# Storing y from ACT's queue in place of SP's in a two-step conditional residual kernel

## The reference, cut to what matters

```
x: (128, 64, 1024) float32; cond ids: (128,) in 0..15; adapter ids: (128,) in 3..7
x = x + einsum('bct,bcd->bdt', x, W0[cond])       # W0[16]: 64 x 64 per condition
x = x + einsum('bsi,boi->bso', x, W1[adapter])    # W1[8]: 1024 x 1024 per adapter
```

## Time and profile before

| what | value |
|---|---|
| median of 3 runs | 861.83 us (860.33 to 862.73) |
| span of the profiled execution | 859.8 us |
| PE matmul | 813.6 us, 95% |
| DVE | 450.2 us, 52% |
| ACT | 279.4 us, 32% |
| POOL | 26.5 us, 3% |
| mean granted TensorE clock | 0.993 |
| DMAs | 90.84 MB, mean 106 GB/s |

### The profile page before, as it was taken

The page is one execution under the profiler, slowest core; times in us unless marked ns, Lnnn a source line. Parts: engine busy times, 40 slices in busy tenths (PEclk is TensorE's granted clock), DMA queues, the critical chain, the costliest instruction groups (busy, mean ns, idle before and its releaser), DMA issues.

```text
span 859.8 us, 17186 instructions
## 1 busy us (share of the span) xinstructions
PE 813.6 (95%) x3572; PEld 666.1 (77%) x3573; DVE 450.2 (52%) x466; ACT 279.4 (32%) x515; POOL 26.5 (3%) x61
## 2 busy tenths in 40 slices
PE   3599999999999999999999999999999999999997
PEld 3478778778777888877778887777888888888885
DVE  5556665566666344656653465666344433444342
ACT  2233233323323333233233323323333223322332
POOL 3100000000000000000000000000000000000000
PEclk9799999999999999999999999999999999999999
DMA  4433333334333323343333233333322322223223
GB/s 143 140 110 106 125 112 123 111 114 128 107 124 116 97 80 99 113 129 106 125 115 98 90 112 126 108 127 108 98 83 81 92 86 86 81 88 90 86 79 88
DMA packets 66655, 90.84 MB, mean 106 GB/s; under 512 B 6228, under 2 KB 57428, under 8 KB 66644
## 3 DMA queue, kind: packets, MB, share of 16 engines
q1 hardware_dynamic: 66644, 90.72, 34.2%
HBM read 57.15 MB, written 33.55 MB: 105 GB/s over the span
## 4 chain that ended last, share of the span: by engine, by line
PE 57%; SPq 18%; issue 7%; DVE 7%; ACT 3%; DMA 3%; DVEq 3%; ACTq 1%; POOL 0%; POOLq 0%
PE z_ps L452 17%; PE z_ps L453 17%; PE z_ps L455 16%; SPq L342 5%; SPq L191 5%; SPq L359 4%; DVE w_turned L700 3%; DVE x_turned L715 2%; SPq L373 2%; PE y_ps L466 2%; PE y_ps L468 2%; PE y_ps L467 2%; DVEq L191 2%; DMA w_nat<-in_L_cond_weight_dram 1%; DMA y<-in_L_cond_weight_dram 1%
## 5 line engine op out<-in xcount | busy, mean ns | idle before, releaser
L452 PE MATMUL z_ps<-w_hi,xt_hi 128*128 (+1 forms) x1056 | 413.3, 391 | 16.7 <-DVE z_lo L740 16.4
L453 PE MATMUL z_ps<-w_lo,xt_hi 128*128 (+1 forms) x1056 | 410.9, 389 | 0.0
L455 PE MATMUL z_ps<-w_hi,xt_lo 128*128 (+1 forms) x992 | 386.1, 389 | 0.0
L452 PEld LDWEIGHTS z_ps<-w_hi,xt_hi 128*128 128x128 f32 x1056 | 198.2, 188 | 66.2 <-issue 25.5
L453 PEld LDWEIGHTS z_ps<-w_lo,xt_hi 128*128 128x128 f32 x1056 | 198.3, 188 | 40.6
L455 PEld LDWEIGHTS z_ps<-w_hi,xt_lo 128*128 128x128 f32 x992 | 186.2, 188 | 38.9
L740 DVE TENSOR_TENSOR z_lo<-z_ps,z_hi 128x512 fp32r<-128x512 f32 x132 | 90.9, 689 | 201.2 <-ACT z_hi L559 200.6
L715 DVE STREAM_TRANSPOSE x_turned<-x_in 128x1024 f32<-128x1024 f32 x67 | 143.9, 2148 | 42.0 <-issue 31.7
L547 ACT ACTIVATE xt_hi<-x_turned 128x1024 fp32r<-128x1024 f32 x67 | 71.1, 1061 | 241.3 <-DVE x_turned L715 241.3
L559 ACT ACTIVATE z_hi<-z_ps 128x512 fp32r<-128x512 f32 x132 | 78.1, 592 | 191.3 <-PE z_ps L455 143.8
L724 DVE TENSOR_TENSOR xt_lo<-x_turned,xt_hi 128x1024 fp32r<-128x1024 f32 x62 | 76.7, 1236 | 69.9 <-ACT xt_hi L547 69.9
(11 more groups left out here) (111 smaller groups left out, 141.7 us busy)
## 6 DMA issues: line engine op xcount, KB each, us to landing
x_in<-in_x_dram SPq DMA_DIRECT2D x272, 128.0 KB
out_dram<-y SPq DMA_DIRECT2D x128, 256.0 KB, 3.1
w_nat<-in_L_cond_weight_dram SPq DMA_DIRECT2D x128, 128.0 KB
w_nat<-in_L_cond_weight_dram SPq DMA_DIRECT2D x4, 512.0 KB, 7.0
w_turned<-in_L_cond_weight_dram SPq DMA_DIRECT2D x2, 512.0 KB, 3.8
y<-in_L_cond_weight_dram SPq DMA_DIRECT2D x2, 512.0 KB, 8.3
x_turned<-in_L_cond_weights_dram SPq DMA_DIRECT2D x2, 256.0 KB, 3.9
ids_i<-in_itok_B_dram SPq DMA_DIRECT2D x2, 0.5 KB, 2.1
```

The lines of the kernel that those rows point to most:

```text
L452: nc.tensor.matmul(z_ps[n][:], xt_hi[h][:, t, :], whi, start=(t == 0), stop=False)
L453: mm = nc.tensor.matmul(z_ps[n][:], xt_hi[h][:, t, :], wlo, start=False, stop=last and not pair)
L455: mm = nc.tensor.matmul(z_ps[n][:], xt_lo[h][:, t, :], whi, start=False, stop=last)
```

## The change

`store_y` leaves SP's program. The same function, with the same look at three fields of the table, the same wait for `y_made` and the same two DMAs, is now issued by ACT as the last step of its slot, behind `keep_z_hi(s, 1)`, and once more behind the last `make_y`. The buffers, the semaphores and the order of everything else stay. SP waits for the last stores as before.

```
             def slot(j, h):
                 s = 2 * j + h
                 load_x(s + 2, h, turned=s + 1)
                 load_chunks(s + 1)
-                if not first:
-                    store_y(j - 1 + h, 1 - h)
...
-            store_y(pairs_past, 1)
...
+            def store_y(s, h):
+
+                a, b, stores = look(act, s, SAMPLE_A, SAMPLE_B, STORES)
+
+                def store(sample, lo):
+                    act.dma_start(out_rows[bass.ds(sample * C, C), :], y[h][lo:lo + C, :]).then_inc(y_stored[h], 16)
+
+                with act.If(stores > 1):
+                    act.wait_ge(y_made, NH * s + NH)
+                    store(a, 0)
+                    store(b, C)
...
                 make_y(before, 1 - h)
                 place_w0_a(s)
                 keep_z_hi(s, 1)
+                store_y(before, 1 - h)
...
             make_y(2 * pairs_past + 1, 1)
+            store_y(2 * pairs_past + 1, 1)
```

More of the change, by code:

```diff
@@ L366, in load_chunks, with slot @@
                             load(1)
[L368 to L389, removed]
+            def slot(j, h):
                 s = 2 * j + h
@@ L402, in _ @@
             sp.wait_ge(first_turned, NH * CHUNKS_PER_GROUP)
-            slot(0, 0, first=True)
+            slot(0, 0)
             slot(0, 1)
@@ L564, in make_y @@
                     nc.scalar.activation(y[h][:, n * HALF:(n + 1) * HALF], y_ps[n][:], ACT.Copy).then_inc(y_made, 1)
+            def store_y(s, h):
[6 more added lines that the diff above has]
+                    store(b, C)
+                with act.Else():
+                    with act.If(stores > 0):
+                        act.wait_ge(y_made, NH * s + NH)
+                        store(a, 0)
+                        act.sem_inc(y_stored[h], 16)
+                    with act.Else():
+                        act.wait_ge(y_made, NH * s + NH)
+                        act.sem_inc(y_stored[h], 32)
             def slot(j, h, before):
```

## The result

The changed kernel takes **852.11 us** (median of 4 runs, 850.5 to 852.12), the kernel before 861.61 in the same comparison (4 runs, 860.33 to 862.73). The ratio is 0.9887, with a 95% interval of 0.9867 to 0.9906: faster by 9.5 us. 854.6 had been predicted.

A forecast was written before the change was run, and what follows sets the result against it. PE bounds the kernel, at work in 95% of the 859.8 us span; 859.8 - 7.6 (stalls) + 0.4 (end) = 852.6, plus 2.0 for the median: 854.6 us. The forecast's own range was 852 to 859, the whole range 850.5 to 863.5.

The forecast's parts named there:

- The rule for the stalls: In chunk slots PE's stall is c - 1.31 less the stall at the slot's own start, or none if negative.
- c: Time from Z to DVE's transpose of x, xt_hi's lateness added: 2.05 us in even (loop-jump) slots, 1.42 + 0.06 in odd.
- The cause of the long look: Any engine's look is long if started from 0.7-0.9 us, until before 2.6, behind a store's first DMA.
- The store's place: ACT issues the store's first DMA at Z + 1.2; DVE's look starts at most 0.1 us behind, taking 0.55.
- Z: Start of z_hi, on ACT, for a slot's second half; the slot's later steps are timed from it.
- ACT's pair of issues: ACT's two DMA issues of a store were taken as 1.32 us, SP's figure; SP's shortest pair was 1.16.
- the rival of the late ACT queue: ACT issues of 1.13 us make xt_hi 1.2 or 1.15 late: 872.2 us; chance 0.17 together with another slower rival.
- xt_hi: ACT's step after DVE's transpose of x: 0.1 us late in even slots, 0.06 in odd; 0.2 added for ACT's look.
- What it said would show: PE's z_lo waits 8 to 10 us over about 20, POOL wait gone, xt_hi at most 0.2 late.
- The sum of the stalls: PE's stalls in chunk slots: 2.96 us per group of eight, 11.8 for four groups against 19.4, gain 7.6.
- The end: After the last piece of y, ACT's look and issue put the last store later: a loss of 0.4 us.
- SP's part: SP loses 2.9 us of 13.27 per chunk slot; the POOL waits for late chunks go, 1.5 us of the gain.

The follow-up runs named there:

- the kernel with both looks late: Changed kernel with DVE's look of chunk bounds moved behind the transpose of x and ACT's behind xt_hi: 840.86 us.
- DVE's look made harmless and the stores on SP: Kernel before, stores still on SP, with DVE's look of chunk bounds moved behind the transpose of x: 857.75 us.
- the same with the stores on ACT: Changed kernel with DVE's look of chunk bounds moved behind the transpose of x: 847.69 us.
- SP relieved and the look hit: Changed kernel with ACT's look for the store moved ahead of z_hi, so the store is issued earlier: 866.76 us.
- ten DMAs: Changed kernel with x of a slot loaded in ten DMAs in place of four, the same bytes: 859.48 us.
- nine DMAs: Changed kernel with x of a slot loaded in nine DMAs in place of four, the same bytes: 858.26 us.

## Why the prediction was right, and where its terms were off

**The rule for the stalls** held in all versions. It said 0.64 for c = 1.95, and 0.65 was measured; for c = 1.24 it says none, and the kernel with both looks late has none.

**The cause of the long look** was right. The looks are long behind a store and in no run without one. That the store's place would spare DVE's look in the kernel after was right too: 0.53 or 0.54 in front of every transpose, c 1.95 in even and 1.42 in odd slots (but for the first two chunk slots, 1.90 and 1.64), both as predicted.

**The store's place** came out at Z + 1.05, where the sum had Z + 1.2: from the look's end to the DMA ACT needs 0.25 us, not the 0.38 taken over from SP. DVE's look starts 0.24 behind the DMA in even slots, not 0.1, still ahead of the stretch.

**ACT's pair of issues** took 1.13 to 1.15 us in 57 of 62 cases (1.26 to 1.58 in the others), its best bound, where 1.32 was taken from SP. An issue is 0.48 us on ACT, a little under the 0.5 to 0.7 that were to show, so the rival of the late ACT queue, which begins at 0.89 with its register work, is excluded. The page "Perfetto Trace Analysis" of the Trainium skill (section "DMA Instruction — HWDGE (DVE, Sync)") has an issue include a wait for a descriptor generator that the sequencers of DVE and Sync share. ACT's 128 issues show little of one: a median of 0.48 and at most 0.70.

**xt_hi** had been forecast 0.1 late in even and 0.06 late in odd slots. It is 0.03 after the transpose in nearly all even slots, thus in time, and 0.20 to 0.34 late in the odd ones (once 0.59), but for the first of each later group, 0.03. The step that was mis-sized is the 0.2 added to ACT's own look, and the place of that look with it: the sum had it 2.2 behind the first DMA. In odd slots the look starts 1.4 behind the first DMA and takes 1.24, against 0.49 undisturbed, so the addition was 0.75; in even slots it starts 1.7 behind and takes 0.94, 0.45 more. That the odd slots still don't stall follows from the rule: c of 1.42 + 0.21 would give 0.32, and the stall of 0.65 in front of it covers that.

**What it said would show** mostly did: PE's waits for z_lo come to 8.3 us and none is above 0.8, though over 15 and not 20; the wait for POOL is gone; the long looks of DVE lie under the transpose. Xt_hi's limit of 0.2 was passed, in odd slots and in two even ones (0.38 and 0.26).

**The sum of the stalls** was 11.8 us and is 8.95. A group's terms as the later groups have them (0.16, 0.38, 0, then three even slots of 0.65) come to 2.5, beside 2.96 predicted and 1.8 to 2.6 measured. That is 1.9 us of the 2.9 by which the prediction was too careful; most of the rest is the first group, with its 1.8. The low end of its range was added up wrongly: with 10.2 us of stalls in place of 11.8 its own sum gives 853.0, not 852.

**The end** cost 1.1 us, not 0.4. In the order of ACT's queue the store of the slot before the last stands between the last z_hi and the last pieces of y:

```profile
842.06 0.60 ACT L535 ACTIVATE z_hi<-z_ps 128x512 fp32r<-128x512 f32 x1 [4.08 <-PE z_ps L431]
...
843.12 1.13 ACTq L547 DMA_DIRECT2D out_dram<-y  x2
...
844.75 1.08 ACT L540 ACTIVATE y<-y_ps 128x512 f32<-128x512 f32 x2 [2.09 <-PE y_ps L444]
846.33 1.13 ACTq L547 DMA_DIRECT2D out_dram<-y  x2
```

The first piece of y starts 2.69 behind z_hi, where it was 0.68 before. So the second starts at 845.24, 1.23 after the last matmul (844.01), against 0.43 before: 0.8 us, and this term was missing. The store's look after it takes 1.14, hit by that earlier store, and the DMA follows the last piece by 1.09 in place of 0.77: 0.3 us, near the 0.4 forecast.

**SP's part** was placed wrongly. The prediction gave it 1.5 us, the waits for POOL that PE saw. The runs show a second limit of nearly the same height behind the first: in the kernel before, PE's stalls of 4.4 to 6.1 us a group stretched a slot to 12.8 to 13.0 us, so that SP's 13.27 took little of its lead and only 3.3 us of waits for POOL showed. The total came out in spite of this because it priced the kernel after, in which neither limit is left. The split did not: by it, a short look with SP left full would have gained some 6 of the 7.6 us. For the term of SP it is luck that the change relieves both at once. Measured from the two sides: with DVE's look made harmless and the stores on SP, 857.75; the same with the stores on ACT, 847.69. That is 10.1 us for SP's part. With SP relieved and the look hit, 866.76. A harmless look alone gives 3.6 us (861.39 - 857.75, with an interval that ends just short of no gain), and a relieved SP gives none while the look is hit; the change gains 9.5 because it does both. The page "DMA: Bandwidth & Descriptors" of the Trainium skill (section "Issuing engines are not separate DMA queues") calls the saved time on the sequencer usually small relative to the DMA itself. Here it is not small: a pair of issues took SP 1.32 us, where a store lands 3.1 us after its issue. With the look and what stands around it 2.9 us leave SP's slot, and that lifts SP from slower than PE to faster.

It is not only the issues' time. A store in SP's queue also waits for y: 110.8 us in 36 waits of SP in the kernel before, of which 33.0 us in 14 waits lie before 600 us, where the chunks are. There are none after, where SP waits for the transpose of x instead (243.0 us). The lead with which a group of chunks begins is 17.8 us in the kernel after (issue at 158.04, turned at 175.88), 13.9 with ten DMAs and 10.7 with DVE's look late and the stores on SP, each read at the start of the second group. The wait by itself does no harm: the run without stores keeps it in SP's queue, drops only the two issues, and no chunk is late. How much of the 10.1 us belongs to the wait and how much to the issue time is not settled, since the runs with nine and ten DMAs scatter by 6 to 9 us and their profiled executions are among the quicker ones.

One more thing changed with the engine: the stores left the loads' DMA queue (q1 on the page before) for one of their own (q10 on the page after). That is not what brings the chunks in time. POOL begins a chunk 6.1 us (median) after its last DMA is issued in the kernel before, 5.9 in the run without stores, 6.0 with ten DMAs and the stores in ACT's queue, and 8.6 in the kernel after.

## What to carry to other kernels

A wait that costs time may hide a second limit of the same height: before pricing the relief of a queue, compare its work per slot (13.27 us) with what the bounding engine would need without its stalls (12.24). A small scalar read from the on-chip buffer in front of critical work belongs behind it, or away from stores: here that is worth 11.1 us on top of the change, for two lines. And a store moved into another engine's queue is paid where that queue has nothing to hide it, here at the very end.

## What the hardware showed beyond expectation

- A read of two fields takes 0.53 us on DVE and 0.49 on ACT, and reads go up to 1.56 and 1.83 in the kernel before while a store out of the on-chip buffer is in flight. A load of the same 256 KB into it leaves every one of DVE's and ACT's at 0.55 or less. The extra time falls with the distance from the first DMA: on ACT 0.75 us at 1.4 behind it and 0.45 at 1.7, in most slots. Four looks at 1.8 to 2.0 have 0.57 to 0.76 more, so that the distance does not say it all.
- A DMA issue of a store takes ACT 0.48 us (median, kernel after), and SP 0.56 for the same store (kernel before). A load of x or of a chunk takes SP 0.54 at best and 0.56 in the median.
- Some of SP's own issues of x and of chunks became slower in the kernel after, up to 1.9 us for one where the kernel before has 0.75 at most in its slots, but for the 1.13 of the earlier trace rows. SP has the time to spare and nothing waits for it; the cause was not looked for.
- Most versions with a full SP queue scatter more from run to run: 855.5 to 861.6 with nine DMAs and 857.8 to 865.0 for the kernel before over 11 runs, against 851.6 to 852.5 and 839.8 to 841.0 with a free one, of which there are only 4 runs each. The version with a load in the store's place has a full queue too and stays within 865.3 to 867.5 over 7 runs. The cause is open.
